# Attention and channel-mix block on one core: another opening, two key blocks a step for the last two groups, score shifts ahead

## The reference

```
x = y
h = layernorm(x)
q, k, v = h@Wq+bq, h@Wk+bk, h@Wv+bv
w = softmax(causal(q @ k.T / sqrt(256)))
x = x + (w @ v) @ Wo + bo
h = layernorm(x);  hp = h shifted down one row (zero row first)
xr, xk = mu_r*h + (1-mu_r)*hp,  mu_k*h + (1-mu_k)*hp
x = x + sigmoid(xr @ W_r.T) * (relu(xk @ W_k.T)**2 @ W_v.T)
```

## Time and profile before

| | us |
|---|---|
| median of 3 runs (lowest, highest) | 389.09 (388.43, 390.05) |
| the profiled execution | 390.67 |
| its span | 388.9 |
| PE busy, share of span | 357.9, 92% |
| PEld | 322.3, 83% |
| DVE | 260.7, 67% |
| ACT | 244.5, 63% |
| POOL | 210.0, 54% |

### The profile page before, as it was taken

How to read it: one execution, slowest core, us unless ns; L and a number is a source line. 1 busy time by engine, 2 the same in 40 slices (tenths; PEclk the granted TensorE clock), 3 DMA queues, 4 the chain that set the end, 5 groups by cost and what they waited for, 6 DMA issues and landing times.

```text
span 388.9 us, 6803 instructions
## 1 busy us (share of the span) xinstructions
PE 357.9 (92%) x2433; PEld 322.3 (83%) x2433; DVE 260.7 (67%) x596; ACT 244.5 (63%) x496; POOL 210.0 (54%) x250
## 2 busy tenths in 40 slices
PE   3798999989899999899999799998999989999885
PEld 3576788979799788789998689987889979999874
DVE  3559596598656796945279678487864477576655
ACT  1134636776587476598533974873768658777973
POOL 1111333456368751869732385742575479589861
PEclk9899999999999999999999999999999999999999
DMA  7600000000002000200030000200000000000101
GB/s 200 205 0 3 0 2 0 3 1 3 27 2 81 2 1 29 82 2 0 2 110 1 2 0 28 83 0 2 1 2 29 1 29 1 29 27 17 41 1 54
DMA packets 11891, 10.66 MB, mean 27 GB/s; under 512 B 1873, under 2 KB 11858, under 8 KB 11858
## 3 DMA queue, kind: packets, MB, share of 16 engines
q1 hardware_dynamic: 11858, 10.23, 8.5%
HBM read 6.04 MB, written 4.19 MB: 26 GB/s over the span
## 4 chain that ended last, share of the span: by engine, by line
PE 49%; DVE 19%; ACT 12%; POOL 10%; issue 7%; DMA 2%; SPq 0%; ACTq 0%; DVEq 0%
PE W L683 10%; PE W L686 10%; PE W L687 10%; PE O L830 5%; PE O L832 5%; PE O L831 5%; DVE mix L601 5%; POOL p_lo L304 3%; DVE peak L557 3%; ACT st L381 2%; DVE xhat L488 2%; ACT mix L399 2%; POOL mix_lo L315 2%; DMA x_in<-in_L_attn_y_all_dram 2%; ACT st L345 1%
## 5 line engine op out<-in xcount | busy, mean ns | idle before, releaser
L304 POOL TENSOR_TENSOR p_lo<-st,p_hi 128x512 fp32r<-128x512 f32 (+1 forms) x94 | 91.7, 995 | 49.1 <-ACT p_hi L345 48.0
L557 DVE TENSOR_TENSOR peak<-peak,W 128x512 f32<-128x512 f32 (+3 forms) x85 | 44.7, 526 | 78.4 <-ACT st L345 76.8
L830 PE MATMUL O<-v_hi,p_hi 128*128 128x258 f32 x272 | 78.8, 290 | 4.3 <-POOL p_lo L304 4.2
L832 PE MATMUL O<-v_hi,p_lo 128*128 128x258 f32 x272 | 76.7, 282 | 0.0
L831 PE MATMUL O<-v_lo,p_hi 128*128 128x256 f32 x272 | 76.4, 281 | 0.0
L683 PE MATMUL W<-xT_hi,kT_hi 128*128 128x512 f32 (+2 forms) x188 | 65.9, 351 | 7.8 <-DVE peak L557 4.3
L381 ACT ACTIVATE st<-st 128x512 f32<-128x512 f32 (+1 forms) x94 | 47.3, 504 | 37.5 <-DVE st L569 37.5
L345 ACT ACTIVATE st<-W 128x512 f32<-128x512 f32 (+1 forms) x94 | 44.3, 475 | 35.9 <-PE W L687 35.5
L686 PE MATMUL W<-xT_lo,kT_hi 128*128 128x512 f32 (+2 forms) x188 | 65.8, 350 | 0.0
L687 PE MATMUL W<-xT_hi,kT_lo 128*128 128x512 f32 (+2 forms) x188 | 63.2, 336 | 0.0
L830 PEld LDWEIGHTS O<-v_hi,p_hi 128*128 128x128 f32 x272 | 51.2, 188 | 6.5 <-POOL p_lo L304 5.9
(11 more groups left out here) (112 smaller groups left out, 764.4 us busy)
## 6 DMA issues: line engine op xcount, KB each, us to landing
x_in<-in_L_attn_y_all_dram SPq DMA_DIRECT2D x8, 512.0 KB, 5.0
out_dram<-gate SPq DMA_DIRECT2D x15, 256.0 KB, 2.1
h_row<-in_L_attn_Wk_dram SPq DMA_DIRECT2D x1, 256.0 KB, 2.8
h_row<-in_L_attn_Wq_dram SPq DMA_DIRECT2D x1, 256.0 KB, 3.2
st<-in_L_attn_Wv_dram SPq DMA_DIRECT2D x1, 256.0 KB, 6.1
st<-in_L_attn_Wo_dram SPq DMA_DIRECT2D x1, 256.0 KB, 6.2
mix<-in_L_ffn_W_k_dram SPq DMA_DIRECT2D x1, 256.0 KB, 4.1
mix<-in_L_ffn_W_r_dram SPq DMA_DIRECT2D x1, 256.0 KB, 4.4
```

The lines of the kernel that those rows point to most:

```text
L304: g.tensor_tensor(p_lo[:, u % NP, r], score_tile(u), p_hi[:, u % NP, r].bitcast(f32), ALU.subtract)\
L557: v.tensor_tensor(peak[:, J % 2, r], peak[:, J % 2, r], scores, ALU.max).then_inc(maxed, 1)
L830: mm(bank_o[q][:, 0:VW], p_hi[:, u % NP, w], v_hi[:, j, :], start=j == 0, stop=False)
L832: last = mm(bank_o[q][:, 0:VW], p_lo[:, u % NP, w], v_hi[:, j, :], start=False, stop=end)
```

## The change

**Loads.** SP issues Wk, Wq, x group 0 in four loads of one tile (each with its own semaphore), Wv, Wo, x group 1, the FFN matrices. The six small loads are issued by ScalarE.

**Weights.** VectorE takes the transposed Wk; ScalarE takes Wq, with the negated first column as its bias; GpSimd copies the bias columns. kT of group 0 is made hi·hi for both halves, then with `wkq_lo`, then with `xT_lo`; its second half has a free O bank.

**Zero products.** `idle(n)` multiplies a zeroed buffer into an unused bank, 22 times in five places.

**Two key blocks a step.** `WIDE` is 2 for the two-tile groups: a step there holds the scores of two key blocks side by side, 512 columns, so they have 7 and 8 steps. Their peaks take twice the transposes. A weighted product waits for its own O bank tile by tile.

**Shifts ahead.** `shift` follows its own table `SUB_AT`, up to four a slot from the slot after the spread on, where before it ran with exp.

**Tables.** All slot tables are new, for 79 steps.

```diff
-    LAST = NJ - 1
-    COUNT = [TG * (G % GB) + t0 + n for G, t0, n in GROUPS]
+    LAST = len(PARTS) - 1
+    WIDE = [TG // n for G, t0, n in GROUPS]
+    COUNT = [(TG * (G % GB) + t0 + n) // (TG // n) for G, t0, n in GROUPS]
     FIRST = [sum(COUNT[:J]) for J in range(NJ + 1)]
-    STEPS = [(J, j) for J in range(NJ) for j in range(COUNT[J])]
+    STEPS = [(J, j * WIDE[J]) for J in range(NJ) for j in range(COUNT[J])]
...
-            elif size == TG // 2 and j % 2:
-                found.append((found[s - 1][0], GW // 2 + cols_of(s).start))
...
-    MT_AT = [(4,), (12,), (24,), (40,), (44,), (52,), (67,), (79,), (131,)]
+    MT_AT = [(4,), (13,), (24,), (40,), (44,), (53,), (65,), (71,), (109,)]
...
-    MB_AT = [(4,), (13,), (24,), (40,), (47,), (53,), (70,), (81,), (134,)]
+    MB_AT = [(5,), (17,), (25,), (40,), (44,), (54,), (68,), (72,), (144,)]
...
+    IDLE = (6, 1, 5, 6, 4)
...
+    SUB_AT = [min(P_AT[u], MB_AT[STEPS[u][0]][0] + 1 + (u - FIRST[STEPS[u][0]]) // 4) for u in range(NS)]
+    SUB_IN = {s: [u for u in range(NS) if SUB_AT[u] == s] for s in SLOTS}
...
+        early = (bank_o + bank_w[:NO - 1:-1])[:4]
...
+            return early[1] if use == ("kT", 0, 1) else bank_w[USES.index(use) % NW]
...
-            with nc.allow_non_contiguous_dma(reason="vectors of 256 numbers, once"):
-                for i, vec in ((BK, bk), (BQ, bq)):
-                    sp.dma_start(cols[:, i, :], vec.rearrange("(k p) -> p k", p=P)).then_inc(qk_loaded, 16)
             sp.dma_start(raw_k, halves(wk)).then_inc(wk_loaded, 16)
             sp.dma_start(raw_q, halves(wq)).then_inc(wq_loaded, 16)
-            load(0)
+            for t in range(TG):
+                sp.dma_start(x_in[:, 0, t, :], y_t[:, t, :]).then_inc(x0_loaded[t], 16)
             sp.dma_start(raw_v, halves(wv)).then_inc(wv_loaded, 16)
             sp.dma_start(raw_o, halves(wo)).then_inc(wo_loaded, 16)
-            with nc.allow_non_contiguous_dma(reason="vectors of 256 numbers, once"):
-                for i, vec in ((BV, bv), (MU_R, mu_r), (MU_K, mu_k)):
-                    sp.dma_start(cols[:, i, :], vec.rearrange("(k p) -> p k", p=P)).then_inc(col_loaded, 16)
-            sp.dma_start(bo_row, bo.rearrange("(a c) -> a c", a=1)).then_inc(bo_loaded, 16)
+            load(1)
             for i, w in enumerate((w_k, w_r, w_v)):
                 sp.dma_start(raw_ffn[:, i], halves(w)).then_inc(ffn_loaded, 16)
-            load(1)
...
+            pool.wait_ge(bias_loaded, 32)
+            g.tensor_copy(wkT[:, :, 0], cols[:, BK, :]).then_inc(bias_ready, 1)
+            g.tensor_copy(wqT[:, :, 0], cols[:, BQ, :]).then_inc(bias_ready, 1)
             rsqrt1(0)
+            pool.wait_ge(col_loaded, 48)
+            g.tensor_copy(wvT[:, :, 0], cols[:, BV, :]).then_inc(bias_ready, 1)
...
+            with nc.allow_non_contiguous_dma(reason="vectors of 256 numbers, once"):
+                for i, vec in ((BK, bk), (BQ, bq)):
+                    a.dma_start(cols[:, i, :], vec.rearrange("(k p) -> p k", p=P)).then_inc(bias_loaded, 16)
+                for i, vec in ((BV, bv), (MU_R, mu_r), (MU_K, mu_k)):
+                    a.dma_start(cols[:, i, :], vec.rearrange("(k p) -> p k", p=P)).then_inc(col_loaded, 16)
+            a.dma_start(bo_row, bo.rearrange("(a c) -> a c", a=1)).then_inc(bo_loaded, 16)
+            sc.wait_ge(fold_ready, 2)
+            high(minus_first[:], pairs(early[1])[:, :, 0], minus_ready, scale=-1.0)
+            sc.wait_ge(minus_ready, 1)
+            for d in range(KC):
+                last = a.activation(wqT[:, d, 1:C], early[1][:, d * C + 1:(d + 1) * C], ACT.Identity, bias=minus_first[:, d:d + 1])
+            last.then_inc(q_taken, 1)
...
-            taken(0, bank_o[0], wkT, BK, qk_loaded, 32)
-            taken(1, bank_o[1], wqT, BQ, qk_loaded, 32)
+            v.memset(warm.bitcast(f32), 0.0).then_inc(warm_ready, 1)
+            taken(early[0], wkT, 1, 0)
...
-            taken(2, bank_o[2], wvT, BV, col_loaded, 48)
             for h in range(KC):
                 xT_part(0, h)
+            taken(early[2], wvT, 4, 1)
+            for h in range(KC):
+                kT_part(0, h)
+            dve.wait_ge(fold_moved, 2)
+            low(wvo_lo[:], early[0][:].rearrange("p (k c) -> p k c", k=KC), wvo_hi[:], fold_split)
+            dve.wait_ge(col_loaded, 48)
             v.tensor_scalar(cols[:, OM_R:OM_K + 1, :], cols[:, MU_R:MU_K + 1, :], -1.0, 1.0, ALU.mult, ALU.add)\
                 .then_inc(om_ready, 1)
             v.memset(hT[:, :, 0:1], 0.0).then_inc(prev_ready, 1)
-            for h in range(KC):
-                kT_part(0, h)
-            dve.wait_ge(fold_moved, 2)
-            low(wvo_lo[:], bank_o[0][:].rearrange("p (k c) -> p k c", k=KC), wvo_hi[:], fold_split)
...
-                for u in P_IN[s]:
+                for u in SUB_IN[s]:
                     shift(u)
...
+                for b in range(WIDE[J]):
+                    r = cols_of(s) if WIDE[J] == 1 else slice(b * n * P, (b + 1) * n * P)
+                    left = min(r.start, r.stop - 2 * P)
+                    stop = (t0 + n) * P
+                    q = slice(stop - (r.stop - left), stop)
+                    keys, mask = slice((j + b) * P, (j + b + 1) * P), None
+                    if diagonal(s, b) >= t0:
+                        at = r.start + (0 if WIDE[J] == 1 else (diagonal(s, b) - t0) * P)
+                        m0 = P if WIDE[J] == 1 or b == 0 else 0
+                        mask = (bank[:, at + m0 - P:at + P], ident_b[:], mask_b[:, m0:])
+                    last = product(bank[:, left:r.stop],
+                                   [(kT_hi[:, k, keys], kT_lo[:, k, keys], xT_hi[:, G % NT, k, q], xT_lo[:, G % NT, k, q])
+                                    for k in range(KC)], mask)
+                last.then_inc(s_ready, 1)
...
                 for t in range(n):
-                    last = nc.tensor.transpose(bank_b[:, t * P:(t + 1) * P], peak[:, J % 2, t * P:(t + 1) * P], ident[:])
+                    for b in range(w):
+                        c = t * w + b
+                        last = nc.tensor.transpose(bank_b[:, c * P:(c + 1) * P], peak[:, J % 2, (b * n + t) * P:(b * n + t + 1) * P], ident[:])
...
+                for b in range(WIDE[J]):
+                    for q in tiles_of(u, b):
+                        tile, o = G * TG + q, o_of(G, q)
+                        if j + b == 0 and tile >= NO:
+                            pe.wait_ge(o_used, tile - NO + 1)
+                        c = (b * n + q - t0) * P
+                        w = slice(c, c + P)
+                        end = diagonal(u, b) == q
+                        mm(o[:, 0:VW], p_hi[:, u % NP, w], v_hi[:, j + b, :], start=j + b == 0, stop=False)
+                        mm(o[:, 0:C], p_hi[:, u % NP, w], v_lo[:, j + b, :], start=False, stop=False)
+                        last = mm(o[:, 0:VW], p_lo[:, u % NP, w], v_hi[:, j + b, :], start=False, stop=end)
...
+            def idle(n):
+                for _ in range(n):
+                    mm(early[3][:], warm[:, 0:P], warm, start=True, stop=True)
+            pe.wait_ge(warm_ready, 1)
+            idle(IDLE[0])
+            pe.wait_ge(const_ready, 9)
             pe.wait_ge(wk_loaded, 16)
-            transposed(raw_k, bank_o[0])
+            transposed(raw_k, early[0])
+            idle(IDLE[1])
             pe.wait_ge(wq_loaded, 16)
-            transposed(raw_q, bank_o[1])
-            pe.wait_ge(taken_ready, 2)
+            transposed(raw_q, early[1])
+            idle(IDLE[2])
+            pe.wait_ge(bias_ready, 2)
+            pe.wait_ge(taken_ready, 1)
+            pe.wait_ge(q_taken, 1)
             for h in range(KC):
                 for d in range(KC):
                     last = mm(bank_b[:, h * C:(h + 1) * C], wkT[:, d, h * P:(h + 1) * P], wqT[:, d, :], start=d == 0, stop=d == KC - 1)
             last.then_inc(fold_ready, 1)
-            pe.wait_ge(wv_loaded, 16)
-            transposed(raw_v, bank_o[2])
+            idle(IDLE[3])
             for h in range(KC):
                 xT(0, h)
-            for h in range(KC):
-                kT(0, h)
-            pe.wait_ge(taken_ready, 3)
+            pe.wait_ge(wv_loaded, 16)
+            transposed(raw_v, early[2])
+            idle(IDLE[4])
+            xh, xl = xT_hi[:, 0], xT_lo[:, 0]
+            pe.wait_ge(xT_high, KC)
+            pe.wait_ge(fold_moved, 1)
+            for w, x, wait in ((wkq_hi, xh, None), (wkq_lo, xh, (fold_split, 1)), (wkq_hi, xl, (xT_split, KC))):
+                if wait:
+                    pe.wait_ge(*wait)
+                for h in range(KC):
+                    for k in range(KC):
+                        last = mm(bank_of("kT", 0, h)[:], w[:, k, h * P:(h + 1) * P], x[:, k, :], start=x is xh and w is wkq_hi and k == 0,
+                                  stop=x is xl and k == KC - 1)
+                    if x is xl:
+                        last.then_inc(kT_ready, 1)
...
```

(4 more changed lines are left out.)

204 lines of the change are left out of this document (101 added, 103 removed).

## The result

The kernel after takes **369.29 us** (median of 4, 369.20 to 369.42). The kernel before took 389.57 in runs made beside it (388.43 to 391.06). The ratio is 0.9455, with a 95% interval of 0.9419 to 0.9491. The change saves about 20 us where 9.0 were forecast.

The account below looks back on a forecast made before the run. The prediction took TensorE, busy 267.00 of 280 us, to bound the long middle. Its terms -4.1 - 2.9 - 2.9 + 0.9, with 0 for shifts and tables, made -9.0 us: 380.1 us against the median 389.09, range 375 to 386.5.

Parts of the forecast that it names:

- Loads, weights, from xhat to the first score: Opening: earlier loads and shorter preparation bring the first score product at 19.3 us and not 22.98; -4.1 us.
- The first softmax: From first score to first spread of the peak: four us of TensorE waiting become 1.2; -2.9 us.
- the zero products don't raise the clock in time: Rival, opening: zero products, fold and transposes run at low pitch, first score at 22.0; 382.8 us, chance 0.10.
- Shifts ahead, and the new tables: Long middle: more slack may recover some idling, bursts ahead of a maximum may cost; 0, ends -5 and +5 us.
- the loss from bursts: Slower rival, middle: four shifts hold VectorE 2.7 us ahead of maxima, so TensorE waits; 393 us, chance 0.07.
- Two key blocks a step: Two-tile groups: 15 steps for 30 save GpSimd time, -2.9 us; eight more transposes cost +0.9.
- The ceiling: Long middle: TensorE bounds it, so changes to other engines can win at most the 13 us it idles.
- More: Rival: the middle's idling falls by 5 of its 13 us as well; 375 us, chance 0.09.

Follow-up runs that it names:

- open_only: The new opening alone, with the order tables, narrow two-tile steps and shift places of the kernel before; 386.39 us, 0.9894 of the kernel before.
- no_zero: The kernel after without its 22 zero products; 369.58 us, 0.9451 of the kernel before.
- new_tail: New opening, shifts ahead, old order for the head, new order with two key blocks a step for the last groups; 382.42 us, 0.9782 of before.
- new_head: New opening, shifts ahead, new order up to weighted step 49 and group 4, old order with narrow steps behind; 390.91 us, 0.9995 of before.
- shifts_8: The kernel after with up to eight shifts in a row behind the spread in place of four; 371.06 us, 0.9503 of before.
- open_shifts: As open_only, with the shifts ahead (new SUB_AT) as the only other edit; 387.45 us, 0.9906 of before.
- open_wide: As open_only, with two key blocks a step in the two-tile groups and the old tables' last slots pressed together; 395.68 us, 1.0155 of before.
- np2_tail: The kernel after with two steps of lookahead in place of three from step 64 on; 383.92 us, 0.9825 of before.

## Why the prediction was wrong in size

**Right.** *Loads, weights, from xhat to the first score*: -4.1 forecast, -3.9 measured (open_only). In part the parts make up for each other: the last x tile landed 1.8 us sooner (6.87 against 8.69) where 1.0 was taken, while starting the statistics before it (6.24) brought 0.7 where 1.05 was. *The first softmax*: -2.9 forecast, -2.5 by TensorE's lost time. The premise of the rival "the zero products don't raise the clock in time" didn't come true, and its price was wrong: no_zero, where the fold does run at the low level, has its first score 0.14 us later, not 2.7. The 0.9 us that the last four zero products were to cost is not there either: without them TensorE waits for xT_hi until 13.46 instead of 13.41.

**The failed step: "Shifts ahead, and the new tables", put at 0 with ends of -5 and +5.** The two were taken as one edit in a middle that was thought nearly full. Between new_tail and the kernel after, which differ in the head's order alone, the last product comes 12.5 us sooner. 2.5 of them are the first softmax counted above, and 10.0 are left: **-10.0** where 0 stood. This is its worth in front of the new last groups; in front of the old ones it is worth nothing (new_head). The waits for the maximum fell from 4.9 us to 0.3 and those for kT_lo from 1.8 to none. The prediction had a fact in its hands that may explain it: "more TensorE work between gather and spread than before in most groups", 13.7 us for 2.1 in the seventh (13.9 for 2.8 in the traces). That this is what ended the waits is my reading; no run moves it alone. Having read both the earlier trace rows, I set the loss from bursts against it without working out either; shifts_8 shows no such loss.

**Mis-sized: "Two key blocks a step".** -2.9 + 0.9 = -2.0 was forecast, from GpSimd's own saving. With the order made for it, and still behind the old head, the last groups bring **-5.0** (open_shifts to new_tail). GpSimd's row came out as forecast (58 of 1306 ns), but that wasn't what it was worth: in the old order the same saving came with a loss of 9 us (open_only to open_wide), and with the same width and less lookahead (np2_tail) 14 us of the change go. The prediction named the lookahead ("three steps of lookahead holding six blocks") and gave it nothing in the sum, and at most 1.8 us, the p_lo waits of the old order.

**The ceiling.** "No change to the other engines can win more than the 13 us that it idles" counted only idling that records show. TensorE's busy time also fell, from 357.9 us to 355.4, while its products by their pitches rose by 6.1: so 8.6 us more of "busy" were lost time in the kernel before than in the kernel after, over the whole kernel: waiting inside modelled ends, and slow products in the opening. By distances between starts the middle before lost 21.2 us, not 13.0 (60 to 340), and the middle after still loses 8.3 (58 to 322). The ceiling was too low by 8 us, and the 12.9 that went would have been all of it.

**The sum.** -3.9 (opening), -2.5 (first softmax), +1 (shifts alone, within the noise), -10.0 and -5.0 are -20.4; the ratio gives 0.0545 x 389.57 = 21.2. The rest is within the intervals. These are the steps of one path (open_only, open_shifts, new_tail, after). By way of new_head the same change would be +3.5 for the head and some -21 for the last groups, so no term has a worth of its own. "More", the nearest rival, named the right place (the middle's idling) and half of its size.

**What stays open.** Which entries of the new tables bring the 10.0 wasn't separated further. new_head and new_tail each have a seam that neither full order has, and what it costs isn't known. None of these variants is faster than the kernel after; no_zero is as fast.

## What to carry to other kernels

Order, lookahead and step width of a hand-scheduled kernel are one design: here in the old order shifts ahead gave nothing and wide steps cost up to 10 us, and the new order without one part cost 26 to 40 us. When a table of slots is rewritten, price it by what stands between a request and its use at every wait in the trace, rather than by what the edited instructions cost; and look for the longest block on each in-order queue (here 6.9 us on GpSimd), because lookahead that reaches over it saved a wait of 6.0 us there and the slow products behind the wait. Take TensorE's idle time from the distance between starts, not from busy time.
